# Cross-attention's odd context row: a mask product and a fifth term of the sum over heads, in place of a four-row matmul

## The reference, cut to what matters

```python
# x: (32, 32, 512)   ctx: (32, 257, 384)   16 heads of 32 channels
q = layernorm(x) @ Wq.T                       # masked rows are scaled to zero
k, v = split(ctx @ Wkv.T)                     # 257 context rows for each of 32 batches
p = softmax(q * 32 ** -0.5 @ k.T)             # per batch and head: 32 queries x 257 rows
x = x + p @ v                                 # per head
```

## Time and profile before

| what | before |
|---|---|
| median of three runs | 1950.63 us |
| profiled execution | 1954.27 us, its span 1952.5 us |
| busy over the span | PE 1586.1 us (81%), DVE 1192.9 us (61%), ACT 711.7 us (36%) |
| attention over the batches | about 54 us to 535 us of the span |
| line 443, PE | 64 records |
| context loads, line 238 | 32 of 385.5 KB, 3.9 us to landing |

### The profile page before, as it was taken

How to read it: one execution, slowest core, us unless ns; L and a number is a source line. 1 busy time by engine, 2 the same in 40 slices (tenths; PEclk the granted TensorE clock), 3 DMA queues, 4 the chain that set the end, 5 groups by cost and what they waited for, 6 DMA issues and landing times. The chain is left out here.

```text
span 1952.5 us, 22186 instructions
## 1 busy us (share of the span) xinstructions
PE 1586.1 (81%) x7269; PEld 1151.5 (59%) x7269; DVE 1192.9 (61%) x2594; ACT 711.7 (36%) x1361; POOL 94.9 (5%) x261
## 2 busy tenths in 40 slices
PE   7999999999899999508700059749999999999998
PEld 3777777777677777403200048646666666666664
DVE  4355455465413677999999936344565555555555
ACT  2333333333244545400000032124555555555552
POOL 0000000000000000002111200030000000000003
PEclk9999999999899999858955559769999999999999
DMA  3211010010025145414100042064335515144104
GB/s 114 78 33 32 16 33 24 25 33 16 0 90 91 54 38 91 84 27 153 43 0 0 0 113 65 1 250 174 135 125 177 195 38 199 67 155 173 38 17 135
DMA packets 116457, 153.06 MB, mean 78 GB/s; under 512 B 47217, under 2 KB 68209, under 8 KB 116369
## 3 DMA queue, kind: packets, MB, share of 16 engines
q1 hardware_dynamic: 110640, 137.81, 23.7%
q0 software_dynamic: 2560, 8.39, 1.3%
q10 hardware_dynamic: 3168, 5.77, 0.8%
HBM read 250.32 MB, written 31.39 MB: 144 GB/s over the span
## 5 line engine op out<-in xcount | busy, mean ns | idle before, releaser
L1686 DVE TENSOR_TENSOR gl<-w_gu,gh 128x2048 fp32r<-128x2048 f32 x138 | 290.8, 2107 | 16.5 <-ACT gh L1621 16.5
L1621 ACT CAST gh<-w_gu 128x2048 fp32r<-128x2048 f32 x138 | 242.2, 1755 | 62.3 <-DMA w_gu<-in_up_proj 52.3
L1576 PE MATMUL bank<-w_d,hT 128*128 128x512 f32 x506 | 245.2, 603 | 13.6 <-ACT hT L1645 13.5
L1553 PE MATMUL bank<-gh,xh 128*128 128x512 f32 (+1 forms) x552 | 219.0, 397 | 10.9 <-DVE xl L1677 9.5
L1719 DVE TENSOR_TENSOR hid<-silu,bank 128x256 f32<-128x256 f32 x138 | 55.1, 399 | 262.9 <-ACT silu L1634 262.9
L1555 PE MATMUL bank<-gh,xl 128*128 128x512 f32 (+1 forms) x552 | 206.8, 375 | 0.0
L1554 PE MATMUL bank<-gl,xh 128*128 128x512 f32 (+1 forms) x552 | 206.6, 374 | 0.0
L1182 PE MATMUL bank<-o_v,xnT 128*128 128x64 f32 x256 | 36.1, 310 | 176.0 <-DMA o_v<-scratch_v_rows 176.0
L1576 PEld LDWEIGHTS bank<-w_d,hT 128*128 128x128 f32 x506 | 92.0, 189 | 88.4 <-issue 56.0
L1182 PEld LDWEIGHTS bank<-o_v,xnT 128*128 128x128 f32 x256 | 35.8, 227 | 176.8 <-DMA o_v<-scratch_v_rows 176.8
L1634 ACT ACTIVATE silu<-bank 128x256 f32<-128x256 f32 x138 | 50.7, 367 | 211.6 <-PE bank L1555 211.4
(11 more groups left out here) (295 smaller groups left out, 3126.0 us busy)
## 6 DMA issues: line engine op xcount, KB each, us to landing
w_gu<-in_gate_proj SPq DMA_DIRECT2D x46, 1024.0 KB
w_gu<-in_up_proj SPq DMA_DIRECT2D x46, 1024.0 KB
w_d<-in_down_proj SPq DMA_DIRECT2D x46, 1024.0 KB
w_gu<-in_gate_proj SPq DMA_DIRECT2D x23, 768.0 KB
w_gu<-in_up_proj SPq DMA_DIRECT2D x23, 768.0 KB
w_d<-in_down_proj SPq DMA_DIRECT2D x23, 768.0 KB
ctx_raw<-in_ctxT SPq DMA_DIRECT2D x32, 385.5 KB, 3.9
scratch_gram<-gram SPq DMA_DIRECT2D x8, 768.0 KB, 3.3
```

The source lines that it names most:

```text
L1553: pe.matmul(bank, xh[s % 2][:, k, :], hi, start=(k == 0), stop=False)
L1576: mm = pe.matmul(bank, hT[n % 2][:, c, :], w_d[:, b * (BLK // P) + c, :], start=(b == 0 and c == 0), stop=(b == NB - 1 and c == cs[-1]))
L1621: nc.scalar.copy(gh[n % RING][:, :, :, 0:bw].rearrange("p k a f -> p (k a) f"), w_gu[:, :, :, b * BLK:b * BLK + bw].rearrange("p k a f -> ...
L1686: nc.vector.tensor_tensor(gl[n % RING][:, :, :, 0:bw].rearrange("p k a f -> p (k a) f"), w_gu[:, :, :, b * BLK:b * BLK + bw].rearrange("p ...
```

## The change

The odd row's probabilities are no longer transposed. DVE spreads them over the token columns instead: `p_tail[(h, n), c, n']` is the probability where n = n', and zero elsewhere (`same_token` is that mask, made once). PE multiplies `p_tail` (128 columns) with `block_mask` as the weights, 128x128: channel r then receives, per channel group and token, the probability of its own head. DVE multiplies this with `v_last`, now kept on chip with channels on partitions, and writes the product as a fifth entry of `o_masked`. The sum over heads takes five terms. The four-row matmul of line 443 goes, with `probT_tail`, the `v_tail` loads and the DRAM copy of `v_last`. A new semaphore, `p_spread`, lets PE start the mask product. `v_last` is computed by 12 matmuls of 32 columns like `k_last`.

```diff
-        v_last = sb("v_last", [B, C])
+        v_last = sb("v_last", [P, KC, B])
+        same_token = sb("same_token", [P, N])
...
-            @block.sync
-            def _(sp):
-                sp.wait_ge(vl_copied, 1)
-                sp.dma_start(d["v_last"], v_last[:, :]).then_inc(vl_out, 16)
...
-                for k in range(KY):
-                    mm = pe.matmul(ps[7][0:B, :], ctx_last[:, k, :], wkv[:, k, C:2 * C], start=(k == 0), stop=(k == KY - 1))
-                mm.then_inc(vl_done, 1)
-                for c in range(KC):
-                    for k in range(KY):
-                        mm = pe.matmul(ps[6][:, c * B:(c + 1) * B], wkv[:, k, c * P:(c + 1) * P], ctx_last[:, k, :],
-                                       start=(k == 0), stop=(k == KY - 1))
-                mm.then_inc(vl_done, 1)
+                for bank, at in ((ps[7], C), (ps[6], 0)):
+                    for c in range(KC):
+                        for k in range(KY):
+                            mm = pe.matmul(bank[:, c * B:(c + 1) * B], wkv[:, k, at + c * P:at + (c + 1) * P], ctx_last[:, k, :],
+                                           start=(k == 0), stop=(k == KY - 1))
+                    mm.then_inc(vl_done, 1)
...
+                nc.vector.tensor_reduce(same_token[:, :], ident[:, :].rearrange("p (h n) -> p n h", n=N), AX.X, ALU.add)
                 dve.wait_ge(vl_done, 1)
-                nc.vector.tensor_copy(v_last[:, :], ps[7][0:B, :]).then_inc(vl_copied, 1)
-
-        attend(nc, d, ps, ident, wkv_hi, wkv_lo, k_last, ctx_hi, ctx_lo, block_mask, qT, oT, vl_out,
+                nc.vector.tensor_copy(v_last[:, :, :].rearrange("p c b -> p (c b)"), ps[7][:, 0:KC * B]).then_inc(vl_copied, 1)
...
-        v_tail = [sb(f"v_tail{s}", [KC, P]) for s in range(4)]
...
-        probT_tail = [sb(f"probT_tail{s}", [KC, KC, P]) for s in range(2)]
+        p_tail = [sb(f"p_tail{s}", [P, KC, N]) for s in range(2)]
...
-        o_masked = sb("o_masked", [P, KC, HG, N])
-        tail_in = [sem(f"tail_in{s}") for s in range(4)]
+        o_masked = sb("o_masked", [P, KC, HG + 1, N])
+        p_spread = sem("p_spread")
...
-                def load_tail(b):
-                    if b >= 4:
-                        sp.wait_ge(o_done, b - 3)
-                    sp.dma_start(v_tail[b % 4][:, :], d["v_last"][b:b + 1, :].rearrange("a (c n) -> (a c) n", c=KC)
-                                 ).then_inc(tail_in[b % 4], 16)
-
                 load_first_weights(sp)
-                sp.wait_ge(vl_out, 16)
-                for j in range(B // 2):
-                    if j:
-                        sp.wait_ge(lo_done, j)
-                        load_context(sp, j)
-                    load_tail(2 * j)
-                    load_tail(2 * j + 1)
+                for j in range(1, B // 2):
+                    sp.wait_ge(lo_done, j)
+                    load_context(sp, j)
...
                         if m == 2:
-                            pe.transpose(ps[5][0:KC, 0:P], prob[s][:, :, M - 1], ident[:, :]).then_inc(t_done, 1)
+                            pe.wait_ge(p_spread, b + 1)
+                            pe.matmul(ps[5][:, 0:KC * N], block_mask[:, :, :].rearrange("p h n -> p (h n)"),
+                                      p_tail[s][:, :, :].rearrange("p c n -> p (c n)"), start=True, stop=True).then_inc(t_done, 1)
                             break
...
-                def apply(b, s, tail, r4):
+                def apply(b, s):
                     pe.wait_ge(t_copied, (b + 1) * 3)
-                    pe.wait_ge(tail_in[tail], (r4 + 1) * 16)
                     if not first(b):
                         pe.wait_ge(o_taken, b)
-                    pe.matmul(ps[7], v_tail[tail][:, :], probT_tail[s][:, :, :].rearrange("e c n -> e (c n)"), start=True, stop=False)
                     for c in range(KC):
                         cols = slice(c * P, (c + 1) * P)
                         for m in range(2):
-                            mm = pe.matmul(ps[7][:, cols], val[s][:, m, cols], probT[s][:, m, cols], start=False,
-                                           stop=(c == KC - 1 and m == 1))
+                            mm = pe.matmul(ps[7][:, cols], val[s][:, m, cols], probT[s][:, m, cols], start=(m == 0), stop=(m == 1))
                     mm.then_inc(o_done, 1)
...
+                    dve.wait_ge(norm_done, b + 1)
+                    if not (isinstance(b, int) and b < 2):
+                        dve.wait_ge(t_done, (b - 1) * 3)
+                    nc.vector.tensor_tensor(p_tail[s][:, :, :], prob[s][:, :, M - 1:M].to_broadcast([P, KC, N]),
+                                            same_token[:, None, :].to_broadcast([P, KC, N]), ALU.mult).then_inc(p_spread, 1)
...
-                    nc.vector.tensor_tensor(probT_tail[s][:, :, :], ps[5][0:KC, 0:P][:, None, :].to_broadcast([KC, KC, P]),
-                                            ident[0:KC, 0:KC][:, :, None].to_broadcast([KC, KC, P]), ALU.mult).then_inc(t_copied, 1)
+                    nc.vector.tensor_tensor(o_masked[:, :, HG, :], ps[5][:, 0:KC * N].rearrange("p (c n) -> p c n", c=KC),
+                                            v_last[:, :, bass.ds(b, 1)].to_broadcast([P, KC, N]), ALU.mult).then_inc(t_copied, 1)
...
-                    nc.vector.tensor_tensor(o_masked[:, :, :, :], ps[7].rearrange("p (c h n) -> p c h n", c=KC, h=HG),
+                    nc.vector.tensor_tensor(o_masked[:, :, 0:HG, :], ps[7].rearrange("p (c h n) -> p c h n", c=KC, h=HG),
```

More of the change, by code:

```diff
@@ L231, in cross_attention @@
         x_in, mask_in = [sem(f"x_in{t}") for t in range(NT)], sem("mask_in")
-        w_in, consts, vl_done, vl_copied, vl_out = (sem("xw_in"), sem("consts"), sem("vl_done"),
-                                                          sem("vl_copied"), sem("vl_out"))
+        w_in, consts, vl_done, vl_copied = sem("xw_in"), sem("consts"), sem("vl_done"), sem("vl_copied")
         wq_in, kl_copied, ctx_in, hi_done, lo_done, wkv_split = sem("xq_in"), sem("kl_copied"), sem("ctx_in"), sem("ctx_hi_done"), sem("ctx_lo_done"), sem("wkv_split")
@@ L326, in _, with attend @@
                         split_lo(0)
+                nc.vector.tensor_reduce(same_token[:, :], ident[:, :].rearrange("p (h n) -> p n h", n=N), AX.X, ALU.add)
                 dve.wait_ge(vl_done, 1)
-                nc.vector.tensor_copy(v_last[:, :], ps[7][0:B, :]).then_inc(vl_copied, 1)
-        attend(nc, d, ps, ident, wkv_hi, wkv_lo, k_last, ctx_hi, ctx_lo, block_mask, qT, oT, vl_out,
+                nc.vector.tensor_copy(v_last[:, :, :].rearrange("p c b -> p (c b)"), ps[7][:, 0:KC * B]).then_inc(vl_copied, 1)
+        attend(nc, d, ps, ident, wkv_hi, wkv_lo, k_last, v_last, same_token, ctx_hi, ctx_lo, block_mask, qT, oT,
                load_context, split_hi, split_lo, ctx_in, hi_done, lo_done, x_nat, stats, load_first_weights)
         second_norm(nc, x_nat, xnT, stats, oT, ident, ps)
-def attend(nc, d, ps, ident, wkv_hi, wkv_lo, k_last, ctx_hi, ctx_lo, block_mask, qT, oT, vl_out,
+def attend(nc, d, ps, ident, wkv_hi, wkv_lo, k_last, v_last, same_token, ctx_hi, ctx_lo, block_mask, qT, oT,
            load_context, split_hi, split_lo, ctx_in, hi_done, lo_done, x_nat, stats, load_first_weights):
@@ L446, in apply, with first_ahead @@
                         for m in range(2):
-                            mm = pe.matmul(ps[7][:, cols], val[s][:, m, cols], probT[s][:, m, cols], start=False,
-                                           stop=(c == KC - 1 and m == 1))
+                            mm = pe.matmul(ps[7][:, cols], val[s][:, m, cols], probT[s][:, m, cols], start=(m == 0), stop=(m == 1))
                     mm.then_inc(o_done, 1)
-                def first_ahead(b, j, slot, tail, r4, tile=None):
+                def first_ahead(b, j, slot, tile=None):
                     values(b + 1, j, (slot, 1))
@@ L458, in first_ahead, with second_ahead @@
                         pe.wait_ge(r_added, tile + 1)
-                    apply(b, 0, tail, r4)
-                def second_ahead(b, j, slot, tail, r4):
+                    apply(b, 0)
+                def second_ahead(b, j, slot):
                     values(b + 1, j + 1, (1 - slot, 0))
@@ L465, in second_ahead @@
                     scores(b + 1, 0, j + 1)
-                    apply(b, 1, tail, r4)
+                    apply(b, 1)
                 values(0, 0, (0, 0))
@@ L470, in _ @@
                 scores(0, 0, 0)
-                first_ahead(0, 0, 0, 0, 0)
-                second_ahead(1, 0, 0, 1, 0)
+                first_ahead(0, 0, 0)
+                second_ahead(1, 0, 0)
                 with pe.Fori(0, B // 4 - 1) as i:
[L474 to L478, removed]
+                    first_ahead(i * 4 + 2, i * 2 + 1, 1)
+                    second_ahead(i * 4 + 3, i * 2 + 1, 1)
+                    first_ahead(i * 4 + 4, i * 2 + 2, 0, tile=i)
+                    second_ahead(i * 4 + 5, i * 2 + 2, 0)
+                first_ahead(B - 2, B // 2 - 1, 1)
                 turn(B - 1, 1, False)
```

(4 more changed lines are left out.)

## The result

| kernel | times, us | ratio to before, 95% interval |
|---|---|---|
| before | median 1950.46 (4 runs) | 1 |
| changed | median 1919.54 (1918.03 to 1923.16, 4 runs) | 0.9839 (0.9824 to 0.9853) |
| changed, again beside its variants | median 1920.63 (5 runs; before 1951.20) | 0.9834 (0.9817 to 0.9851) |

The forecast was 1921.2 us, faster. One of the nine runs of the kernel before beside the second timing took 3251.67 us and stays out of its ratio. The span of the profiled execution fell from 1952.5 to 1921.4 us, by 31.1; the first record behind the attention (line 174) moved from 536.1 to 503.1.

The account below looks back on a forecast made before the run. PE was taken to bound the attention, with DVE setting the even places. Savings of 13.8 (odd), 11.8 (even), 0.9, 1.1 and 1.9 (batches 30, 0, 31), less 0.1 at the start, made 29.4 us: 1950.6 to 1921.2, range 1914 to 1931.

Parts of the forecast that it names:

- Odd places: Applies of odd batches 1 to 29, where PE sets the time: 0.92 us saved at each of 15, 13.8 us.
- Even places: Applies of even batches 2 to 28, where DVE sets the time: 0.84 us saved at each of 14, 11.8 us.
- the sum +0.23: DVE's sum over heads: reading 640 elements instead of 512 adds 0.23 us, the surplus taken as per element.
- "+0.34" for `p_tail`: DVE's chain in even places: p_tail, waiting for normalize, starts the next operation 1.48 instead of 1.14 us after line 544.
- Batches 30 and 31: The last two applies: 0.9 us saved at 30, where PE sets the time, 1.9 at 31, a serial chain.
- "+0.1" for v_last's narrow passes: Ahead of the batches: 24 passes of 32 columns instead of 6 of 512, 2.9 instead of 2.8 us.
- Rival 3: Clock falls behind PE's waits in even places with a residual, 4.6 us lost each; seven give 1953 us; chance 0.03.
- The two rules: Skill rules for DVE: free waits would gain even places 1.8 us in all; slow stepped reads make the fifth term +0.23.
- the row's 0.13: DVE in even places: waiting on the operation before costs 0.04 + 0.09 = 0.13 us, read from the profile's rows.
- 1: Rival: small operations are dear, an even place gains 0.03 to 0.6 us, an odd one 0.6; 1934 us; chance 0.13.
- 4: Rival: the change brings nothing, the apply waits just as long for something else; 1950 us; chance 0.02.
- rival 2: A free longer sum and cheap wait shorten DVE's chain in even places; 35 us gained, 1915 us; chance 0.10.

Follow-up runs that it names:

- e3: The kernel before the change without line 443, the odd row's values left out of the output and everything else kept; 1912.37 us in one run.
- e6: The changed kernel with the mask product done twice; 1924.76 us in one run.
- e4: The changed kernel with four terms instead of five in the sum over heads, the odd row left out of the output; 1915.03 us, ratio 0.9817.
- e1: The changed kernel with the 24 narrow passes of v_last moved ahead of the fifth query projection; 1914.59 us, ratio 0.9810.
- e9: The changed kernel with the edits of e1 and e2 together; 1910.25 us, ratio 0.9786.
- e10: e9 with the split of the next context (split_hi, split_lo) moved from the even place into the odd one before it; 1900.63 us, ratio 0.9733.
- e2: The changed kernel with p_tail made behind spread_queries instead of right behind normalize; 1912.93 us, ratio 0.9807.
- e7: The changed kernel with o_masked laid out so that the five terms lie side by side; 1919.70 us, ratio 0.9835.

## Why the prediction was right

The changed kernel's gain is made at the predicted places: 30.9 us between the medians, for 29.4. The mechanism was right, but that the total lies so near is in part luck. The places behind the first apply gave 31.5 us where 28.4 were forecast, and the start took back 2.5 us more than forecast in one profile and 3.9 in the other.

- **Odd places.** 0.92 us each was forecast, 1.02 came: line 443 was worth 1.18 us, not the 1.05 between its start and line 447's, and the product costs 0.16, not 0.13 (e3; e6 has 0.22 for a second one). In the kernel before the scores' eight passes were followed after 1.84 us, in the changed one after 1.75; line 443 had held something before its own start too (0.09 us of the 1.18). 15 x 1.02 = 15.3 us instead of 13.8.
- **Even places.** DVE's chain sets them, as forecast; e4 and e6 show it from both sides. The chain's terms were right: the sum +0.23 (1.315 us, forecast 1.31), `p_tail` and the spread in size. With a residual the chain from take_out to the spread grew from 8.64 to 8.86 us, +0.22 for +0.19. What wasn't in the sum: the gap from DVE's end to the first pass fell from 0.24 to 0.06 us, and the apply that opens the chain shows its first pass 0.11 us later against its end (1.98 instead of 2.09 us to take_out). So these places gained 1.09 us, not 0.84. At the loop's jump 0.40 us went against it, and the gain was 0.70. That step failed: "+0.34" for `p_tail` was read off places where an operation of 1.23 us had covered the jump. At batch 2 the loop's entry took 0.09 us in the same way. All fourteen: 1.01 + 6 x 0.70 + 7 x 1.09 = 12.8 us, forecast 11.8.
- **Batches 30 and 31.** 1.09 and 2.28 us, forecast 0.9 and 1.9.
- **The start.** "+0.1" for v_last's narrow passes was the worst-sized term. 48 in a row brought the clock down: with batch 0's gain, the first apply was to start its line 431 at 76.5, and it started at 78.96, with 80.37 the second time. e1 gives it back, e9 and e10 a good part of it. How much it costs varies between executions, and the start of the kernel before can have a fall too, of 3.4 us (e3).
- **The clock behind the even places.** Rival 3 feared a fall there, and the prediction held against it that "1.64 us of waiting leaves the stretch at 0.99 now". That reading was wrong: the 0.99 has two falls in it, behind two of the seven waits of 1.64 us. Each cost 1.62 us, not 4.6, since it lasted 3.4 us and not 9. In the changed kernel these waits are 1.54 us and no fall followed; but none followed the waits of 1.64 us in e3 either, so that the change has spared the falls isn't shown.
- **One execution.** The profile of before has two odd places of 19.66 us instead of 18.04: 3.2 us from the two falls of the clock. That execution was 3.8 us above the median of its runs, which fits falls that the others hadn't, but only this one has a trace. Without them the attention gained 15.3 + 12.8 + 1.1 + 2.3 us less the 1.5 or 2.9 us by which its first apply starts later, 30.0 or 28.6. With them it is 33.2 in the first profile, near the 33.0 us of line 174; the parts behind it took 2 us more in the changed kernel's, which was its slowest run. The medians' 31 us have the interval of the ratio around them, 28.7 to 34.3.
- **The two rules.** A wait on the operation ahead isn't free, against what "VectorE: DVE Perf Modes" of the Trainium skill says in section "The DRAIN you can't avoid": e2 puts it at 0.11 us at the start it delays, and at 0.18 in all, near the row's 0.13. And the sum's surplus is per element with a large step (e7). The rule of the 16-byte line in the Trainium skill ("SBUF — State Buffer", section "Door 1: The DMA port swizzle") agrees with it, at steps of 128 and of 20 bytes; where between 4 and 20 bytes the surplus sets in was not tried.
- **Rivals.** 1 and 4 are out by the intervals, 2 by the sizes, 3 by the granted clock of the changed kernel's two profiles from 62 us to the last batch; e10 shows that what rival 2 hoped for was there, 1.0 us more in an even place, behind VectorE.

## What to carry to other kernels

Sort the repeated places by which engine sets them before adding up a saving: the same pass was worth its whole length in odd places and was traded against VectorE's additions in even ones, and a 0.2 us operation costs nothing or 0.2 us by where it stands. A mean of the granted clock near 1.00 can hide short falls: look for repeated places that are longer than their like. A short operation put last in a loop body, or right behind the one it waits for, costs more than its row (0.40 and 0.18 us here): put an independent longer one between. And once one engine's chain sets a place, look for work in it that has room in the neighbouring place: moving the split of the next context, 1.75 us of VectorE's chain, gained about a third of what the whole change did.

## What was not expected of the hardware

- With 48 passes of 32 columns in a row, TensorE busy all the while, the granted clock fell from 1.00 to 0.50 at about 51 or 52 us and came back some 7 to 10 us later in the changed kernel's two profiles. With 24 behind wide work it stayed at 1.00 in e1 and in the kernel before, and fell for 3.4 us in e3, e9 and e10.
- Behind two of seven waits of 1.64 us in the kernel before, the granted clock fell to 0.50 for 3.4 us, which cost 1.62 us each time.
- VectorE's jump to the start of its loop body leaves a hole of 0.4 us behind an operation of 0.29 us and none behind one of 1.23 us.
- A product of 128 columns takes GpSimd 0.70 us where VectorE takes 0.29, and slows a 1536-column operation of VectorE beside it from 1.75 to 1.96 us.
- Writing 512 elements with a step of 20 bytes takes 1.13 us instead of 0.69.
